# Latent attention: three reciprocals in step 9, the fourth in step 10, and the latent output in step 12 instead of step 14

## The reference, cut to what matters

```python
c_q = _rmsnorm(x @ Wq_down, q_norm_w)
q = (c_q @ Wq_up).reshape(b, s, H, HD).transpose(0, 2, 1, 3)
q_rope = _apply_rope((x @ Wq_rope).reshape(b, s, H, RD), cos, sin)
c_kv = _rmsnorm(x @ Wkv_down, kv_norm_w)
k = (c_kv @ Wk_up) ...; v = (c_kv @ Wv_up) ...      # H = 16 heads
k_rope = _apply_rope((x @ Wk_rope).reshape(b, s, H, RD), cos, sin)
scores = (einsum(q, k) + einsum(q_rope, k_rope)) * (HD + RD) ** (-0.5)
attn = softmax(scores, axis=-1)
out = einsum('bhqk,bhkd->bhqd', attn, v)
out = out.transpose(0, 2, 1, 3).reshape(b, s, H * HD) @ Wout
```

## Time and profile before

| | us |
|---|---|
| median of 3 runs | 2155.03 |
| lowest, highest | 2154.64, 2156.91 |
| the profiled execution | 2154.63 |
| its span | 2152.9 |
| latent attention, sequence 1: pairs 0 to 6, from step 9 of pair 0 | 1139 to 1505 |
| end of pair 6 and pair 7 | 1505 to 1585 |
| latent attention, sequence 2: pairs 0 to 6, from step 9 of pair 0 | 1652 to 2020 |

### The profile page before, as it was taken

The page is one execution under the profiler, slowest core; times in us unless marked ns, Lnnn a source line. Parts: engine busy times, 40 slices in busy tenths (PEclk is TensorE's granted clock), DMA queues, the critical chain, the costliest instruction groups (busy, mean ns, idle before and its releaser), DMA issues. The chain is left out here.

```text
span 2152.9 us, 29698 instructions
## 1 busy us (share of the span) xinstructions
PE 1960.6 (91%) x8876; PEld 1279.2 (59%) x8876; DVE 1253.0 (58%) x2704; ACT 822.5 (38%) x1549; POOL 889.0 (41%) x708
## 2 busy tenths in 40 slices
PE   5899958999999789986779999999889999999987
PEld 5676635555655757655646555555566656565566
DVE  6322264666775722227667777777656777777526
ACT  2122243555655212223324444444514444444413
POOL 0344410343223044432026655666425555665732
PEclk9999967999999589997679999999999999999999
DMA  9111241111110811124232212222032222221001
GB/s 395 52 62 64 57 130 30 31 44 32 44 30 1 353 59 60 66 68 166 45 81 56 55 46 52 55 58 58 19 70 59 55 59 59 58 52 46 24 0 52
DMA packets 64617, 150.91 MB, mean 70 GB/s; under 512 B 14320, under 2 KB 19648, under 8 KB 62208
## 3 DMA queue, kind: packets, MB, share of 16 engines
q1 hardware_dynamic: 54240, 120.44, 19.6%
q0 software_dynamic: 9120, 24.92, 3.7%
q10 hardware_dynamic: 1152, 4.19, 0.5%
HBM read 68.95 MB, written 18.61 MB: 41 GB/s over the span
## 5 line engine op out<-in xcount | busy, mean ns | idle before, releaser
L1858 POOL TENSOR_TENSOR mla_PS<-mla_PS,mla_PT 128x1024 f32<-128x1024 f32 x192 | 457.5, 2383 | 232.6 <-ACT mla_PT L2142 225.3
L2142 ACT ACTIVATE mla_PT<-PS 128x512 f32<-128x512 f32 x512 | 297.2, 600 | 390.9 <-PE PS L1962 322.9
L2275 DVE TENSOR_REDUCE mla_MXP<-PS 128x1 f32<-128x512 f32 x512 | 320.9, 679 | 94.9 <-PE PS L1943 94.4
L1971 PE MATMUL PS<-mla_PT,mla_CN 128*64 128x512 f32 x1024 | 249.4, 607 | 2.3 <-ACT mla_PT L2142 2.3
L1283 DVE TENSOR_REDUCE att_MX<-PS 128x1 f32<-128x512 f32 (+3 forms) x304 | 194.2, 660 | 89.7 <-PE PS L994 49.3
L522 DVE COPY moe_HT<-PS 128x256 f32<-128x256 f32 x188 | 70.4, 415 | 299.9 <-PE PS L648 299.9
L2287 DVE RECIPROCAL PS<-PS 128x128 f32<-128x128 f32 x128 | 114.9, 936 | 180.4 <-PE PS L1978 180.4
L1962 PE MATMUL PS<-mla_QH,mla_KH 113*128 113x512 f32 x512 | 216.1, 422 | 0.9 <-ACT mla_PT L2142 0.9
L684 POOL DMA_INDIRECT moe_XS<-rows_in,moe_GI x96 | 93.7, 976 | 266.1 <-PE PS L634 130.8
L1943 PE MATMUL PS<-mla_KH,mla_QH 113*128 113x512 f32 x512 | 184.8, 429 | 20.6 <-DMA mla_KL<-mla_SL 14.0
L1962 PE MATMUL PS<-mla_QL,mla_KH 113*128 113x512 f32 x512 | 202.4, 395 | 0.0
(11 more groups left out here) (295 smaller groups left out, 3175.8 us busy)
## 6 DMA issues: line engine op xcount, KB each, us to landing
W<-in_W_dram SPq DMA_DIRECT2D x16, 2048.0 KB, 28.1
mla_QH<-mla_SH SPq DMA_DIRECT2D x64, 128.0 KB, 2.4
mla_KH<-mla_SH SPq DMA_DIRECT2D x64, 128.0 KB, 2.4
mla_QL<-mla_SL SPq DMA_DIRECT2D x64, 128.0 KB, 2.4
mla_KL<-mla_SL SPq DMA_DIRECT2D x64, 128.0 KB, 2.4
mla_KH<-mla_SH SPq DMA_DIRECT2D x64, 96.0 KB, 2.3
mla_KL<-mla_SL SPq DMA_DIRECT2D x64, 96.0 KB, 2.4
sums_Y<-rows_out SPq DMA_DIRECT2D x9, 512.0 KB, 6.3
```

Of the source, the lines that this page charges most:

```text
L1858: pool.tensor_tensor(PS[:, :], PT[:, slot(0), :] if k == 1 else PS[:, :], PT[:, slot(k), :], ALU.add).then_inc(s_ps.handle, 1)
L1971: ins = pe.matmul(bank(6)[h * DKVL:(h + 1) * DKVL, :], CN[:, b, k, 0:DKVL], PT[:, slot(k), h * HB:(h + 1) * HB], start=(k == 0), stop=(k = ...
L2142: act.activation(PT[:, slot(k), h * HB:(h + 1) * HB], bank(st_bank(s, h))[:, :], ACT.Exp, scale=MLA_SCALE).then_inc(s_p.handle, 1)
L2275: dve.tensor_reduce(MXP[:, n // NPC, c, h, t:t + 1], bank(piece_bank(n))[:, :], AX_X, ALU.max).then_inc(s_mx.handle, 1)
```

## The change

On DVE, for the first block of every pair: step 9 takes three reciprocals (column groups 2, 3 and 0) instead of two; the fourth (group 1) moves from step 13 to step 10, between that step's second and third maximum; group 0 leaves step 11; the latent output moves from step 14 to step 12, between the second and third maximum. Nothing is added or removed: the same instructions stand in another order, in all 16 pairs.

```diff
@@ -2323,7 +2323,7 @@
                             if after and s == ROWS_AT:
                                 latent_rows(after)
                             if s == 9:
-                                reciprocals(2 * it, (2, 3))
+                                reciprocals(2 * it, (2, 3, 0))
                             maxima(near, todo[:2])
                             if s == 2 and not last:
                                 lows(it + 1, 0, (0, 1))
@@ -2334,9 +2334,9 @@
                                 if not last:
                                     products(it + 1, 1, 0)
                                     rotated(it + 1, 1)
-                            if s in (11, 13):
-                                reciprocals(2 * it, (s // 2 - 5,))
-                            if s == 14:
+                            if s == 10:
+                                reciprocals(2 * it, (1,))
+                            if s == 12:
                                 latent_out(2 * it, r, 0)
                             maxima(near, todo[2:])
                             if s == 13 and not last:
```

## The result

The changed kernel takes 2165.93 us (median; 2163.79 to 2170.53) against 2155.03 before: slower by 10.9 us, a ratio of 1.0053 (95% interval 1.0040 to 1.0066). The forecast was slower by 16.4, 2171.0, with a range from 2162 to 2179. The profiled execution has a span of 2164.9 us, 12.0 more than before.

The account below looks back on a forecast made before the run. PE was taken to set the pace, so DVE's order costs only through PE's waits: 14 x (0.81 + 0.53 - 0.53) = 11.3, plus 1.7 and 3.4, is 16.4 us on 2154.6, giving 2171.0 us, range 2162 to 2179.

Parts of the forecast that it names:

- What bounds it: Pairs 0 to 6: PE sets the pace, busy 363.44 of 366 us, waiting only for DVE's maxima, once a pair.
- Third reciprocal hidden, 0.24 to spare: Step 9: DVE's wait of 1.05 us before piece 0 covers the added 0.81 us; cost nothing.
- Fourth reciprocal, +0.81 a pair: Step 10: delays maximum 2, so PE gets piece 5 in step 11 0.70 us late, plus 0.11 for starting again.
- Output, +0.53 and -0.53: Latent output costs PE 0.53 us a pair in step 12, and its leaving step 14 returns 0.53.
- Steps 11 and 13 relieved, worth nothing: Reciprocals leaving these steps gain nothing, since DVE idles afterwards, 1.00 us before piece 8 and 0.20 before piece 16.
- Pair 7, +1.7: Sequence 1: two more reciprocals ahead of the next queries' rotation lengthen PE's wait from 1.51 to 3.2 us, once.
- The clock behind it, +3.4: After pair 7's longer wait the granted clock falls for 8 us, costing PE 3.4 us; bounds 0 and 3.4.
- step-10 term: PE's loss from the fourth reciprocal placed in step 10: 0.81 us a pair forecast, 0.45 at the range's low end.
- (a): Rival: DVE's idle time before pieces 0 and 8 hides the moved work, step 14 is relieved; faster, 2148.9 us; chance 0.05.
- (b): Rival: block maximum, held by POOL's adds, keeps step 15's wait, 14 x 0.53 us more, 2178.4 us; chance 0.08.
- (c): Rival: no difference; fourth reciprocal hidden, output's wait only moves, pair 7's 1.7 us remain, 2156.3 us; chance 0.05.
- (d): Rival: granted clock falls at each new wait, costing up to 14 x 3.4 = 48 us, 2219 us; chance 0.02.

Follow-up runs that it names:

- pair 7 as before: Changed kernel, but pair 7 of sequence 1 has reciprocals and output in the order of the kernel before; 2165.31 us, ratio 1.0056 to the kernel before.
- both in odd steps: Changed kernel with the fourth reciprocal moved to step 11 and the latent output to step 13; 2145.66 us, ratio 0.9968 to the kernel before.

## Why the prediction was right, step by step

- **What bounds it**: right. PE sets the pace in pairs 0 to 6, and every gain and loss there is a wait of a piece for a maximum; the granted clock stayed at 1.00 in them.
- **Third reciprocal hidden, 0.24 to spare**: right to the hundredth (DVE's 0.24 us of idle time before piece 0).
- **Fourth reciprocal, +0.81 a pair**: 0.76. **Output, +0.53 and -0.53**: 0.57 and -0.53. The sum of 0.81 a pair is 0.77 by PE's stretches, 10.7 us for 11.3. No second wait followed in step 11, although only 0.06 us were to spare.
- **Steps 11 and 13 relieved, worth nothing**: right; DVE idles 1.78 us instead of 1.00 there.
- **Pair 7, +1.7**: 1.5, by the chain that was named.
- **The clock behind it, +3.4**: this term was mis-sized. It was 1.5 in the profiled execution by the starts of PE's instructions (1.7 by the granted clock); it had been taken from one row at its full size. Over the six executions with a wait of 2.32 us or more in pair 7 it was 0, 2.6, and four times 1.5 to 1.6, so a middle of the two bounds would have been the better choice.
- **What the sum had not**: the clock behind the earlier wait, untouched by the change, gave 1.6 us back in this execution. Of the 4.4 us by which the sum of 16.4 exceeds the span's 12.0, the clock behind pair 7's wait makes 1.9, the one behind the earlier wait 1.6, the fourteen pairs 0.6; pair 7's wait and all that lies outside these stretches make about 0.2 each.
- **The range**: it held the median, 2165.93, partly by luck. Both values of the forecast, 2171.0 with the clock's fall and 2167.6 without, lie above that. The room below them had been given for a smaller step-10 term (0.45), and that term was nearly full size (0.76); what used the room, in the profiled execution, was the clock behind the earlier wait.
- **Rivals.** (a) is out for this change, but half right in another place: the idle time before pieces 0 and 8 does take such work, if it stands ahead of the first maximum or in the odd step before; then 0.6 us a pair come back, where it reckoned 0.53. (b), the block maximum, was held 1.41 us and ended at 1328.79, when the add of POOL that had started before it ended (1328.77). That is as the rule from the Trainium skill, SBUF — State Buffer, "Who interferes with whom", has it. It had 0.34 to spare against 0.23 reckoned. (c) is out. (d): two waits of 0.76 and 0.57 us a pair left the clock at 1.00 over 1139 to 1505. The Trainium skill, TensorE: Matmul & The Clock Gate, "A second HAM failure mode: psum-queue depth-cycling", tells of a kernel whose clock swings because of short idling between groups of matmuls; these waits did not bring that about:

```profile
1139.00:1505.00 366.00, 359.67 (x1495) 213.14 (x1494) 266.25 (x395) 160.41 (x288) 221.48 (x103) 1.00 0.22 53
```

## What to carry to other kernels

DVE is only 58% busy here, and what one of its instructions costs is decided by its place. Write down for each gap in its queue what the next consumer needs and by when (here 0.18 us in one gap, 1.0 in the next), and put loose work where the idle time stands ahead of it, not behind the first items of a burst that another engine drains through few buffers. Price a wait by the distance between the starts of the waiting engine's instructions, compared with the same place without a wait; the idle time shown is less (0.26 for 0.53 us lost), or none. Where medians of a few runs can't tell two kernels apart, compare such distances over one repeated stretch. Where a work item is moved along a loop body, look at the outer pairs too, where something else stands behind it.

## What the runs showed of the hardware

Behind waits of like length the granted clock fell in some executions and not in others. The rows are 8 us from about the end of PE's wait in pair 7, in the kernel with the fourth reciprocal in step 11 (wait of 2.32 us), in that with both in odd steps (2.32), and in that with the output in step 14 (3.00):

```profile
1561.00:1569.00 8.00, 7.87 (x33) 5.32 (x35) 4.13 (x7) 2.47 (x5) 6.51 (x3) 1.00 0.68 158
...
1554.00:1562.00 8.00, 7.93 (x27) 5.77 (x28) 2.96 (x5) 2.41 (x5) 4.98 (x3) 0.79 0.67 156
...
1564.00:1572.00 8.00, 6.67 (x17) 4.12 (x18) 1.46 (x3) 2.47 (x5) 3.47 (x2) 0.57 0.67 155
```

So none, 1.7 and 3.4 us of clock are missing: it goes down to 1.2 GHz for none, some or most of the stretch. PE lost 0, 1.6 and 2.6 us by it, counted by pair 7's stretch in the table, less that of the kernel before and less what the wait is longer by. The last is less than 3.4 because there the clock fell while PE still waited: it was 0.59 from 1564 to 1565, all of it wait, and 0.50 from 1565 to 1571. Behind the waits of 1.51 us (the kernel before, pair 7 as before, and two reciprocals in step 11) it was 1.00. The earlier wait of 2.59 us is the same in all ten kernels; over 8 us there the clock was 0.57 in three executions and 0.79 in seven, and pair 7's stretch from step 0 to step 9 was 45.3 us in the three and 43.7 to 43.8 in the seven. What decides between these sizes is not settled here.

The clock goes with the 3 to 9 us by which executions of one kernel differ: of the eight of the kernel with the output first in step 12, the three shortest (2142.4 to 2144.9 us) have a mean granted clock of 0.944 or 0.945, the other five (2147.1 to 2151.0) 0.941 or 0.942. Not all of the spread lies in the latent attention: the denominators of its pair 0, step 9, start between 1131.9 and 1137.2 us in the ten traces, though no instruction ahead of them differs. Why is open.
